# Sparse feed-forwards and gated scan of a two-layer model as one block of eight passes, with fp32 down products

## What is computed

```python
def _sparsify_2to4(h):              # of each 4 neighbours the 2 largest stay
    ...
    _, idx = jax.lax.top_k(a, 2)
    mask = (pos == idx[..., 0:1]) | (pos == idx[..., 1:2])
    return (g * mask.astype(g.dtype)).reshape(B, S, I)
def _L1_ffn_ref(x, w_gate, w_up, w_down):
    h = jax.nn.silu(x @ w_gate) * (x @ w_up)            # 256 -> 1024
    return _sparsify_2to4(h) @ w_down                   # 1024 -> 256
def _L1_attn_b_ref(x, W_act, W_val, W_rec):             # the gated scan
    ct = jnp.concatenate([shifted, x], axis=-1)
    re, im = pairs of jax.nn.sigmoid(jax.nn.relu(ct @ W_act.T))
    m = jax.lax.cummax(jnp.sqrt(re * re + im * im), axis=1)
    kv = jax.lax.associative_scan(cmul, (re / m, im / m), axis=1)
    r = jax.nn.sigmoid(jax.nn.relu(ct @ W_rec.T))
    return (kv @ W_val.T) * r ** 4
x = x + _L1_ffn_ref(_layernorm(x), ...)
x = x + _L1_attn_b_ref(_layernorm(x), ...)
x = x + _L1_ffn_ref(_layernorm(x), ...)
```

## Time and profile before

| | us |
|---|---|
| median of 3 runs | 1751.46 |
| the profiled execution | 1762.21 |
| its span | 1760.4 |
| around the span | 1.8 |
| busy in the span: PE, DVE, ACT, POOL | 1428.9, 1118.1, 633.4, 328.4 |
| TensorE clock granted, mean | 0.874 |

### The profile page before, as it was taken

How to read it: one execution, slowest core, us unless ns; L and a number is a source line. 1 busy time by engine, 2 the same in 40 slices (tenths; PEclk the granted TensorE clock), 3 DMA queues, 4 the chain that set the end, 5 groups by cost and what they waited for, 6 DMA issues and landing times. The chain is left out here.

```text
span 1760.4 us, 22917 instructions
## 1 busy us (share of the span) xinstructions
PE 1428.9 (81%) x8400; PEld 1023.4 (58%) x8400; DVE 1118.1 (64%) x2196; ACT 633.4 (36%) x1172; POOL 328.4 (19%) x256
## 2 busy tenths in 40 slices
PE   4899999588999667999768999885799777058996
PEld 3556555377888556888633444333578644046885
DVE  6555444387775567788375556734577658975766
ACT  1354444253333123333215555661433223013331
POOL 1110000163333002433221311000132300001223
PEclk9799878589999888999868999995899888568998
DMA  7622500220000000000032202001000000000000
GB/s 150 87 38 38 73 2 8 74 66 1 1 1 1 0 1 1 1 1 1 31 45 46 46 1 46 2 1 72 1 1 0 0 0 0 1 0 1 1 24 24
DMA packets 20968, 38.97 MB, mean 22 GB/s; under 512 B 4432, under 2 KB 6224, under 8 KB 20360
## 3 DMA queue, kind: packets, MB, share of 16 engines
q1 hardware_dynamic: 20872, 37.70, 11.2%
HBM read 14.54 MB, written 2.10 MB: 9 GB/s over the span
## 5 line engine op out<-in xcount | busy, mean ns | idle before, releaser
L1611 DVE TENSOR_REDUCE attn_negm<-ps 128x2 f32<-128x1024 f32 (+3 forms) x256 | 256.2, 1021 | 118.8 <-PE ps L1250 60.3
L1460 ACT ACTIVATE attn_probs<-ps 128x512 f32<-128x512 f32 (+3 forms) x512 | 237.1, 515 | 206.8 <-PE ps L1273 125.4
L787 POOL TENSOR_TENSOR moe_h_low<-moe_h,moe_h_high 128x512 fp32r<-128x512 f32 x96 | 138.0, 1439 | 327.6 <-ACT moe_h_high L737 327.6
L1264 PE MATMUL ps<-attn_qs,attn_ks 49*128 49x512 f32 (+4 forms) x512 | 159.7, 437 | 37.2 <-ACT attn_probs L1460 34.8
L1240 PE MATMUL ps<-attn_ks,attn_qs 48*128 48x512 f32 (+4 forms) x512 | 124.2, 482 | 21.7 <-DMA attn_ks<-attn_part_low 17.0
L754 ACT ACTIVATE moe_silu<-ps 128x512 f32<-128x512 f32 x96 | 57.4, 598 | 228.6 <-PE ps L660 228.5
L1264 PEld LDWEIGHTS ps<-attn_qs,attn_ks 51*128 51x128 f32 (+1 forms) x512 | 75.5, 203 | 103.7 <-ACT attn_probs L1460 94.8
L1288 PE MATMUL ps<-attn_probs,attn_va 128*32 128x512 f32 (+3 forms) x1024 | 133.5, 599 | 0.0
L1240 PEld LDWEIGHTS ps<-attn_ks,attn_qs 50*128 50x128 f32 (+1 forms) x512 | 53.6, 206 | 90.6 <-issue 60.0
L423 POOL TENSOR_TENSOR mlp1m_kept_low<-mlp1m_h,mlp1m_kept_high 128x512 fp32r<-128x512 f32 x32 | 43.4, 1388 | 304.0 <-ACT mlp1m_kept_high L393 304.0
L810 DVE TENSOR_TENSOR moe_h<-moe_silu,ps 128x512 f32<-128x512 f32 x64 | 43.5, 687 | 56.9 <-PE ps L667 39.3
(11 more groups left out here) (336 smaller groups left out, 3728.9 us busy)
## 6 DMA issues: line engine op xcount, KB each, us to landing
attn_qs<-attn_part_high SPq DMA_DIRECT2D x64, 128.0 KB, 4.8
attn_qs<-attn_part_low SPq DMA_DIRECT2D x32, 128.0 KB, 4.5
attn_ks<-attn_part_high SPq DMA_DIRECT2D x32, 128.0 KB, 5.7
attn_ks<-attn_part_low SPq DMA_DIRECT2D x16, 128.0 KB, 6.9
out_x<-x SPq DMA_DIRECT2D x4, 512.0 KB, 2.6
x<-in_x SPq DMA_DIRECT2D x1, 1536.0 KB, 9.9
attn_qs<-attn_mT SPq DMA_DIRECT2D x64, 4.0 KB
moe_raw<-in_f_gate SPq DMA_DIRECT2D x2, 512.0 KB, 6.2
```

The lines of the kernel that those rows point to most:

```text
L787: pool.tensor_tensor(hc.low[:, j % RING, :], h[:, j % RING, :], hc.high[:, j % RING, :], ALU.subtract).then_inc(low_done, 1)
L1264: last = pe.matmul(ps[:, SC + k, 0:width2(kt)], ks[e:e + ROWS2, b % 2, key_tile(hd), kt * P:(kt + 1) * P], qs[e:e + ROWS2, b % 2, hd // 2, ...
L1460: act.activation(pr[:, s2 % RING, j, 0:n], ps[:, SC + k, 0:n], ACT.Exp, scale=HD ** -0.5).then_inc(exp_done, 1)
L1611: dve.tensor_reduce(m, ps[:, 2 * half:2 * half + 2, 0:width1(qt)], AX, ALU.max, negate=True).then_inc(r1_free, 1)
```

## The change

The five blocks become one, `feed_forward_and_scan`, named "tail". It has 8 passes of 8 chunks: pass 0 to 3 is the first feed-forward of rows 0 to 3, pass 4 to 7 the second. Chunk n (0 to 63) stands in slot n of 73 slots; every engine walks through the slots, and tables `pe_at`, `act_at`, `pool_at` and `dve_at` say what else it does in each. The scan of row b starts in slot s = 15 + 8b and spreads over s to s + 15, so the scans of two rows overlap. Down products follow their chunk by 7 slots.

What else differs:

- The down products use the fp32 h and the fp32 weight as they are: 4 fp32 products of 256 columns a chunk in place of 12 in fp32r. L393 and L423 go, as do the cut and the halves of the down weight. Down has one pair of PSUM banks, so the first of a pass waits for the addition of the pass before. The scan and the transposes share the other two banks, 6 and 7, in turn.
- The comparisons are three instructions of 1536, 1024 and 512 columns with one operand broadcast, the additions four of 1024 columns.
- The scan is per row: `level` 7 times, `tree` 6 times with distances 1 to 32, `fill` once. A complex product is two multiplications that take both parts together and two sums.
- The sigmoid is written as a tanh, which needs no other table than silu; clamping and powers of r move to ACT as relu and squares. The square root still loads its table, and the next silu loads its own back.
- POOL normalises all rows but the first; DVE makes the statistics.
- The gate, up and down weights are loaded in six pieces of 512 KB during the second attention; its own weights move to the other end of SBUF. They are cut at the head of the new block by ACT and POOL in four parts.
- There are no hardware loops; all slots are written out.

The diff, cut to its core:

```diff
-def sparse_feed_forward(nc, name, g, w_gate, w_up, w_down, cut, out=None):
...
-            def down(b, half):
-                    pe.wait_ge(x_done, b + 1)
-                for r in range(4):
-                    pe.wait_ge(low_done, 4 * m + r + 9)
-                    for t in range(NT):
-                        for k, (hp, wp) in enumerate(products(kept, w_down)):
-                            last = pe.matmul(ps[:, 4 + 2 * (b % 2) + t // 2, (t % 2) * D:(t % 2 + 1) * D], hp[:, j, t * P:(t + 1) * P],
-                                             wp[:, j, :], start=j == 0 and t % 2 == 0 and k == 0,
-                                             stop=j == FC - 1 and k == 2, skip_group_check=True)
...
-                for r in range(4):
-                    act.activation(kept.high[:, 4 * half + r, :], h[:, 4 * half + r, :], ACT.Copy).then_inc(high_done, 1)
...
-                    pool.wait_ge(high_done, FC * b + j + 1)
-                    pool.tensor_tensor(kept.low[:, j, :], h[:, j, :], kept.high[:, j, :], ALU.subtract).then_inc(low_done, 1)
...
-                    for (lo, hi), out in cmp_.items():
-                        c.do(dve.tensor_tensor(out[:, :], mag[:, half, lo, :], mag[:, half, hi, :], ALU.is_ge))
...
+def feed_forward_and_scan(nc, name, g, raw, w_down, scan, out):
...
+    DOWN_LAG = 7
+    def scan_from(b):
+        return FC * (b + 1) + DOWN_LAG
...
+        s = scan_from(b)
+        dve_at[s].append(("stats", "s", b))
+        pool_at[s].append(("normalise", "s", b))
+        pe_at[s + 2] += [("row", "s", b, c) for c in range(DC)]
...
+        dve_at[s + 7] += [("divide", b)] + [("level", b, i) for i in (1, 2, 3)]
+        dve_at[s + 8] += [("level", b, i) for i in (4, 5, 6, 7)]
...
+    jobs = Turns([6, 7])
...
+            def down(m):
+                p, j = m // FC, m % FC
+                if j == 0:
+                    at_least(pe, x_done, p)
+                pe.wait_ge(sel_done, m // QUAD + 1)
+                for t in range(NT):
+                    last = pe.matmul(ps[:, DOWN + t // 2, (t % 2) * D:(t % 2 + 1) * D], h[:, j, t * P:(t + 1) * P], w_down[:, j, :],
+                                     start=j == 0 and t % 2 == 0, stop=j == FC - 1, skip_group_check=True)
+                last.then_inc(down_done, 1)
...
+            for n in range(SLOTS):
+                if n < CHUNKS:
+                    chunk(n)
+                if 0 <= n - DOWN_LAG < CHUNKS:
+                    down(n - DOWN_LAG)
+                for job in pe_at[n]:
+                    do(job)
...
+            def square(b):
+                cs.start(b)
+                act.wait_ge(free["act"], jobs.count[("act", b, 1)])
+                cs.step(act.activation(z[:, :, :], z[:, :, :], ACT.Tanh, scale=0.5))
+                act.activation(sq[:, :, :], z[:, :, :], ACT.Square, bias=halfone[:, 1:2]).then_inc(sq_ready, 1)
...
+                for t in range(NT):
+                    last = pool.tensor_scalar(xn[kind][:, t, :], x[:, row0 + t, :], m[:, c0 + t:c0 + t + 1], y[:, c0 + t:c0 + t + 1],
+                                              ALU.add, ALU.mult)
+                last.then_inc(xn_ready[kind], 1)
...
+                cx.do(dve.tensor_tensor(a, part(slice(0, 2)), carry(0), ALU.mult))
+                cx.do(dve.tensor_tensor(e, part(slice(0, 2)), carry(1), ALU.mult))
+                cx.sync()
+                cx.do(dve.tensor_tensor(part(0), a[:, 0], e[:, 1], ALU.subtract))
+                cx.do(dve.tensor_tensor(part(1), a[:, 1], e[:, 0], ALU.add))
...
+            def level(b, i):
+                multiply(lambda k: seg[:, k, :, i], lambda k: seg[:, k, :, i - 1].unsqueeze(1).broadcast_to([P, 2, NS]), (NS,))
+            def tree(b, d):
+                multiply(lambda k: seg[:, k, d:NS, S1 - 1],
+                         lambda k: seg[:, k, 0:NS - d, S1 - 1].unsqueeze(1).broadcast_to([P, 2, NS - d]), (NS - d,))
...
+                dve.tensor_tensor(r4[:, m, :], ps[:, jobs.bank[job], :], r4[:, m, :], ALU.mult).then_inc(free["dve"], 1)
+                dve.wait_ge(free["dve"], jobs.count[job])
+                xb = x[:, NT * b + 2 * m:NT * b + 2 * m + 2, :]
+                dve.tensor_tensor(xb, xb, r4[:, m, :].rearrange("p (t d) -> p t d", t=2), ALU.add).then_inc(x_scanned, 1)
...
+                dve.wait_ge(silu_done, n + 1)
+                dve.wait_ge(up_ready, n + 1)
+                at_least(dve, down_done, n - FC + 1)
+                dve.tensor_tensor(h[:, n % FC, :], sg[:, n % 2, :], ps[:, 2 * (n % 2) + 1, :], ALU.mult).then_inc(prod_done, 1)
...
+                    for lo, first in ((0, 0), (1, 3), (2, 5)):
+                        n = 3 - lo
+                        c.do(dve.tensor_tensor(ge[:, first:first + n, :], mag[:, lo, :].unsqueeze(1).broadcast_to([P, n, T]),
+                                               mag[:, lo + 1:4, :], ALU.is_ge))
...
+                    c.do(dve.tensor_tensor(cnt[:, 0:2, :], ge[:, 0:4:3, :], ge[:, 1:5:3, :], ALU.add))
+                    c.do(dve.tensor_tensor(cnt[:, 2:4, :], ge[:, 1:5:3, :], ge[:, 3:6:2, :], ALU.add))
+                    c.do(dve.tensor_tensor(cnt[:, 0:4:3, :], cnt[:, 0:4:3, :], ge[:, 2, :].unsqueeze(1).broadcast_to([P, 2, T]), ALU.add))
+                    c.do(dve.tensor_tensor(cnt[:, 1:3, :], cnt[:, 1:3, :], ge[:, 0:6:5, :], ALU.subtract))
...
+                    for r, (level, op) in enumerate([(1.5, ALU.is_ge), (0.5, ALU.is_ge), (0.5, ALU.is_le), (1.5, ALU.is_le)]):
+                        hr = h[:, (QUAD * q + r) % FC, :]
+                        c.do(dve.scalar_tensor_tensor(hr, cnt[:, r, :], level, hr, op, ALU.mult))
...
+            for n in range(SLOTS):
+                p = (n - DOWN_LAG) // FC - 1
+                if (n - DOWN_LAG) % FC == 0 and 0 <= p < PASSES:
+                    add_to_x(p)
+                if n < CHUNKS:
+                    product(n)
+                q, part = n // QUAD - 1, n % QUAD
+                if 0 <= q < CHUNKS // QUAD and part < 3:
+                    select(q, part)
...
+                for job in dve_at[n]:
+                    do(job)
...
+            pieces = [(sb[n][:, k * h:(k + 1) * h, :], a[n][:, k * h:(k + 1) * h, :], arrived["ffn1"])
+                      for n in [*ffn1, "f1_down"] for h in [a[n].shape[1] // 2] for k in range(2)]
+            attention(nc, "attn1", g, w_of("a1_", att1), False, load_later=pieces)
+        high_end.close()
+        feed_forward_and_scan(nc, "tail", g, w_of("f1_", ffn1), sb["f1_down"], w_of("s_", scan), out)
-        attention(nc, "attn1", g, w_of("a1_", att1), False)
-        halves = place_halves(ffn1, stack)
-        sparse_feed_forward(nc, "mlp0", g, *halves.values(), cut=[(a[n], halves[n]) for n in ffn1])
-        gated_scan(nc, "scan", g, sb["s_act"], sb["s_val"], sb["s_rec"], "scan")
-        sparse_feed_forward(nc, "mlp1", g, *halves.values(), cut=[], out=out)
```

More of the change, by code:

```diff
@@ L8 @@
 from contextlib import ExitStack
+from itertools import islice
 import concourse.bass as bass
@@ L2052, in stages @@
         clear_semaphores()
-        sb.update(place(scan, stack))
+        sb.update(place([*scan, "f1_down"], stack))
         with nc.Block() as block:
```

857 lines of the change are left out of this document (379 added, 478 removed).

## The result

The changed kernel takes 1688.17 us (median of 4, 1675.01 to 1698.98), the kernel before 1754.59 (median of 4, 1744.29 to 1766.39). The ratio is 0.9614, with a 95% interval of 0.9569 to 0.9659: faster by 3.9%. The forecast was 1657, 5.4% faster; the time lies inside the range of 1612 to 1712, 31 us above the forecast.

The account below looks back on a forecast made before the run. PE (367 us) and DVE (377) were taken as about equal, the bound changing by slot. Stretches of 9.3, 60, 48, 219, 53, 41 and 22 make 452 in place of 547; execution 1667.3, median 1657, range 1612 to 1712.

Parts of the forecast that it names:

- the signs that I named: Marks of being right: fp32 down records 0.216 apart, first gate about 1223, periods 70 to 76, DVE over 85%, clock above 0.85.
- B: Rival, all slots: engines mesh, DVE's prices 10% lower, PE bounds; periods of 56, 60 us less, median 1597; chance 0.12.
- C: Rival, slots 15 to 54: PE's clock falls in waits and stays low; 192 us more, 1859, slower than before; chance 0.03.
- A: Rival: DVE dearer through unpacked additions, two-part access patterns and POOL felt in full; 40 us more, median 1697; chance 0.2.
- Head: Block start to first gate product: block change, statistics, normalising, transposes, copy and semaphores take 9.3 us, 32.9 before.
- Slots 0 to 14: First fifteen slots: PE bounds, 57.7 us plus 2.3 while the clock starts at half, 60.
- Slots 15 to 22: First half of row 0's scan: PE 47.1 us, DVE 42, with a small wait 48.
- Periods: Slots 23 to 46, three periods of eight slots: DVE 64.4 us against PE 55, with waits 73 each, 219.
- Slots 47 to 54: Eight slots after the three periods: DVE 51 us plus one wait of 2, 53.
- Slots 55 to the end: Slots 55 to 63 on PE 41 us, then last masks, downs, addition and transfer 22.
- Down at 1.73 a chunk: Four fp32 down products cost PE 1.73 us a chunk against 1.44: dearer by 0.29, 18.5 over 64 chunks.
- POOL in a period: POOL normalises two rows a period; its eight instructions cost DVE 4.1 us, half in idle time, so 2.

Follow-up runs that it names:

- The first run: Changed kernel with POOL's four weight-cutting subtractions moved behind the first row's normalisation; ratio to the kernel before 0.9503, first cutting to end 470.1 us.
- the second run: Changed kernel with DVE's statistics of rows 1 to 3 moved ahead of the first product; ratio to the kernel before 0.9558, first cutting to end 470.3 us.

## Why the prediction was right, and where it was off

**The form was right.** DVE's share decides the middle; PE waits longest for the addition to x, and in a period next longest for the fill; the mean clock doesn't fall (0.93 in the periods). Two of the signs that I named were missed: the first gate product came at 1229.4 us, not at about 1223, and DVE was busy for 82% of a middle period, not for over 85.

**The size was off by two things.** Of the 31 us, 21 are the span of the profiled execution (1686.8 against 1665.5), taken apart below. The other 10 are the 0.6% by which I lowered the forecast because the median of before lay that far under its profiled execution. The changed kernel's median, 1688.17, doesn't lie under its own, 1688.58: that correction was for the chance of one execution.

**The prices were right.** In the changed kernel the comparisons take 1752, 1219 and 685 ns, and the three 3.49 us from first start to last end (3.45 forecast). Additions take 0.69 us for 1024 bf16 elements where POOL stands, against 1.22 for the comparison of as many fp32 ones, so the packed mode is kept; four with their wait take 2.62 (2.65). A level takes 1.16 to 1.17 (1.17), the fill 3.2 (3.3), the reciprocal 3.35, the scan of 512 elements 1.38 (1.25). DVE's own work in a period was 61.9, not 64.4. The fp32 down records stand 0.22 us apart, as forecast.

**The rivals.** B (PE bounds all, periods of 56) fell by the addition to x, which keeps PE standing, and by waits of DVE's that B had at none. C fell by the clock; what I said against it, that the waits in the feed-forwards of before are up to 3 us, was misread: each has one of 8.2 us for POOL too, at a mean clock of 0.93 and 0.92. A had the size (a median of 1697), by causes that it didn't name: the additions were packed, a level took 1.17, POOL cost 0.4 us a period.

**Term by term**, forecast and measured (the last column is mine from the products):

```
                    forecast   measured
head to first gate      9.3      16.9
first gate to 15       60        71.5
slots 15 to 22         48        54.3
three periods         219       214.7
slots 47 to 54         53        58.3
slots 55 to 63, end    63        58.5
sum                   452.3     474.2
```

- **Head, +7.6.** The step that failed is "weights are in SBUF, and ACT's and POOL's cutting of the first half ends at 6". I counted when the cutting ends, not what it does to DVE meanwhile, though the earlier trace rows had shown me the two engines beside each other. The first run shows it: the four instructions lose 7.5 us beside POOL, and the head falls by 6.2, since POOL is late in its turn.
- **Slots 0 to 14, +11.5**, of which 4.7 lie between the first gate product and product 0, a stretch that my "15 x 2.72 + 8 x 1.73 + 3 x 1.04 = 57.7" left out: it counted to a PE that had begun, while DVE's product comes a chunk and a silu later. DVE's statistics of rows 1 to 3 behind product 0, which I had put into DVE's sum ("15 for the first rows") and not into the stretch, are 4.1 net by the second run. It leaves 67.4, and in that are two things that I had at nothing: PE's wait of 3.0 for the first masks, and a clock of 0.5 for some us behind it, which costs 2.8 where it comes ("2.3 while the clock starts at half" has one slow start only).
- **Slots 15 to 22, +6.3.** "47.1, DVE 42: with a small wait 48" takes the larger of two sums. The stretch changes its bound inside. PE leads up to product 20, at 1332.18, 31.2 us behind product 15 at 1301.0 (from its prices, 5 x 4.45 + 1.04 + 7.0 = 30.3). From there DVE goes without a wait for 23.1 us to product 23 at 1355.31. The two are 54.3. The run without levels bears out that the second part is DVE's (51.0).
- **Periods, -4.3.** That the total was near is in part luck, since errors cancel. DVE's work was 2.5 less per period and its wait 4.0 more (9.7, not 5.7), and the 1 for a slow start and the 2 for POOL, which measured 0.4, covered the rest. I had priced the value products' chain at 4.7, "an activation gate, 3.5, and the next chunk, 2.7", and had ACT at nothing; it was 5.4. By the timeline the chunk's gate products end at 1468.0 and ACT's tanh and square hold the silu back for another 1.4; the run with the gate's earlier place shows that the chain made the wait, but moves PE's and ACT's part together. The other 2.3 is the first product behind the addition to x, which waits for PE's down, chunk and silu.
- **Slots 47 to 54, +5.3.** "One wait of 2" was 11.3: 6.9 for PE behind the addition to x, 2.6 for the value products, 1.4 for PE's up products, and twice 0.2. The first is the same wait as the period's 2.3. It is longer here, probably since no levels of another row stand in DVE's slot: in the run without levels it is 6.8 in the middle period too. The addition's earlier place took 4.1 of it away.
- **Slots 55 to the end, -4.5.** From product 55 to 63 there are eight slots, and 8 x 4.45 = 35.6 is what they took (36.3). The addition and the first down, which I had added, lie ahead of product 55, and the 2 us of slow clock there didn't come: it was granted in full (1.00). At the end, where I had added 2 more, it was 1.00 too, but that is chance: behind the same wait three of the later runs have 0.93 and 1.6 us more.
- **Down at 1.73 a chunk, ACT's and POOL's work gone for it**: right. It costs some 3 us in all by the run with three fp32r products, and no more than 6.
- **POOL in a period.** I charged 4.1 us, half of it in the idle. POOL's four instructions take 2.16 us where DVE stands idle, and 4.41 beside DVE's additions; DVE's two instructions there take 0.88 and 0.93 in place of 0.69. So it was mostly POOL that waited, and DVE lost 0.4 us a period, not 2.

## What to carry to other kernels

Where two engines wait for each other in a loop, neither the larger sum nor a taken-out piece tells the bound: cut the loop at each point at which the lead changes, and add the pieces. List the waits of both engines for one period, and remove them in pairs: a wait that hides another makes the first edit look worthless. Small instructions of DVE beside long ones of POOL may have to be priced by the other's length, not their own, as in this head. And before a piece of a profile is compared with the same piece of another, compare the clock that PE was granted in both.

## What was not expected of the hardware

- DVE instructions on four elements took 1.46, 2.26, 2.26 and 2.25 us beside POOL's 128x1024 subtractions of 2.34, and 0.17 without them. The Trainium skill (SBUF — State Buffer, Who interferes with whom) has this as an exclusive lock of the shared ports, for two-input instructions and for those in a 2-port mode, with the one issued first holding it; three of these four are `TENSOR_SCALAR`. The trace agrees in that each waits for the end of one of POOL's; in which mode the three ran no run here shows. The three quarters that I took from the earlier trace rows came from long instructions side by side; how the lock falls there no run here takes apart.
- The same wait of 2.96 us before the first down products was followed by a mean clock of 0.71, 0.83 or 1.00 over 10 us, also where the program up to there is the same (0.71 in the changed kernel, 1.00 without the levels and with the gate's earlier place). It makes 2.8 us. What decides it stays open.
- The part ahead of the block, the same code in every kernel, began its last layers at times from 1198 to 1228 us. ACT's first instruction of the second attention stands at 850.8 to 873.4 in the same profiles, and from there to the block it takes 345.5 to 356.0, so most of that difference arose before the attention. What causes it stays open; it is why gains of 4 us were read from the tail and not from the total.
